# One batch of one-hot rows moved from VectorE to ScalarE, and low products of one layer put last

## The reference

```python
var = jnp.mean(x * x, axis=-1, keepdims=True)
xn = rms_w * (x * jax.lax.rsqrt(var + EPS))
gate = xn @ wg_W + wg_b + (genre_embed @ gg_W + gg_b)
gate_w = jax.nn.softmax(gate, axis=-1)
topk_w, topk_i = jax.lax.top_k(gate_w, TOP_K)
cw = jnp.sum(jax.nn.one_hot(topk_i, E, dtype=x.dtype) * topk_w[..., None], axis=-2)
h1 = jax.nn.relu(jnp.einsum('bsh,ehm->bsem', x, W1) + b1)
h2 = jax.nn.relu(jnp.einsum('bsem,emn->bsen', h1, W2) + b2)
out_e = jnp.einsum('bsen,enh->bseh', h2, W3) + b3
return jnp.einsum('bseh,bse->bsh', out_e, cw)
```

## Time and profile before

| | us |
|---|---|
| median of 3 runs | 443.59 |
| lowest, highest | 442.25, 444.49 |
| profiled execution | 443.45 |
| its span, first to last instruction | 441.5 |
| TensorE busy in it | 406.7 (92%) |
| VectorE, ScalarE, GpSimd busy | 316.5, 294.2, 256.4 |

### The profile page before, as it was taken

One profiled execution on the slowest core, in us unless ns is written; L12 is line 12 of the kernel. 1 busy time (PEld: TensorE's weight loads), 2 busy tenths in 40 slices (PEclk: granted clock), 3 DMA queues, 4 the chain that ended last, 5 costly groups with the idle time before them and its releaser, 6 DMA issues.

```text
span 441.5 us, 12798 instructions
## 1 busy us (share of the span) xinstructions
PE 406.7 (92%) x4134; PEld 365.5 (83%) x4134; DVE 316.5 (72%) x628; ACT 294.2 (67%) x625; POOL 256.4 (58%) x276
## 2 busy tenths in 40 slices
PE   6904989999999999999999999999999999999992
PEld 5604988888888888888888888888888899888891
DVE  3799989849859759769578587555566767776651
ACT  5903798969779789788887865555555556565441
POOL 4740650776676674675656756855556666455324
PEclk9955699999999999999999999999999999999998
DMA  8996499976866756454557454444345443322322
GB/s 281 359 280 208 137 388 383 266 172 167 185 91 158 181 98 150 74 97 70 82 91 171 79 79 74 75 83 76 65 73 78 69 77 71 63 38 37 54 25 33
DMA packets 60968, 57.83 MB, mean 131 GB/s; under 512 B 42059, under 2 KB 55437, under 8 KB 58733
## 3 DMA queue, kind: packets, MB, share of 16 engines
q1 hardware_dynamic: 43072, 38.85, 30.0%
q0 software_dynamic: 13632, 18.00, 25.9%
q10 hardware_dynamic: 4205, 0.17, 0.6%
HBM read 40.08 MB, written 17.83 MB: 131 GB/s over the span
## 4 chain that ended last, share of the span: by engine, by line
PE 68%; ACT 4%; DVE 3%; DMA 3%; issue 2%; POOL 1%; DVEq 1%; POOLq 0%; ACTq 0%
PE bank L1395 49%; PE y_banks L1472 16%; ACT area L837 2%; DMA area<-x_ext,tab_from 2%; PE bank L1375 2%; DVE area L1127 1%; DMA out<-area,tab_to 1%; DVE area L1125 1%; DVE stage L1152 1%; ACT area L863 1%; POOL out L669 1%; PE y_banks L1459 1%; DVEq L1150 0%; ACT w_hi L781 0%; ACT area L851 0%
## 5 line engine op out<-in xcount | busy, mean ns | idle before, releaser
L1395 PE MATMUL bank<-area,w_hi 128*128 128x256 f16 x1248 | 206.3, 273 | 0.0
L1395 PE MATMUL bank<-area,w_lo 128*128 128x256 f16 x624 | 170.1, 273 | 0.0
L669 POOL DMA_INDIRECT out<-area,tab_to x71 | 124.6, 1755 | 63.2 <-issue 22.9
L851 ACT ACTIVATE area<-bank,cprm 128x256 f32<-128x256 f32 (+1 forms) x256 | 127.8, 557 | 43.4 <-PE bank L1395 43.2
L1125 DVE CAST area<-area 128x512 f16<-128x512 f32 (+1 forms) x144 | 65.9, 458 | 95.8 <-ACT area L851 83.6
L1395 PEld LDWEIGHTS bank<-area,w_hi 128*128 (+1 forms) x1248 | 122.1, 98 | 14.3 <-issue 0.2
L631 POOL DMA_INDIRECT area<-x_ext,tab_from x71 | 82.0, 1155 | 52.1 <-issue 36.5
L1127 DVE TENSOR_TENSOR area<-area 128x512 f16<-128x512 f32 (+1 forms) x144 | 99.6, 692 | 5.0
L1472 PE MATMUL y_banks<-w_hi,area 128*128 (+1 forms) x504 | 88.0, 273 | 2.2 <-DVE area L1127 2.2
L863 ACT ACTIVATE area<-area,cw 128x256 f32<-128x256 f32 x71 | 32.2, 499 | 63.3 <-DVE area L1132 44.4
L1472 PE MATMUL y_banks<-w_lo,area 128*128 (+1 forms) x252 | 68.7, 273 | 0.0
(11 more groups left out here) (216 smaller groups left out, 468.0 us busy)
## 6 DMA issues: line engine op xcount, KB each, us to landing
stage<-in_weights SPq DMA_DIRECT2D x10, 1024.0 KB, 5.5
area<-in_x SPq DMA_DIRECT2D x8, 512.0 KB, 8.4
x_ext<-in_x SPq DMA_DIRECT2D x8, 512.0 KB
out<-in_x SPq DMA_DIRECT2D x8, 512.0 KB, 13.1
w_lo<-in_weights SPq DMA_DIRECT2D x4, 1024.0 KB, 8.9
w_hi<-in_weights SPq DMA_DIRECT2D x2, 1024.0 KB, 8.0
area<-x_ext,tab_from POOLq DMA_INDIRECT x71, 3.3
out<-area,tab_to POOLq DMA_INDIRECT x71
```

What stands on the lines that cost most here:

```text
L669: pool.indirect_dma_start(out=out, out_offset=bass.IndirectOffsetOnAxis(ap=tab_to[:, i * SUB + u:i * SUB + u + 1].bitcast(U32), axis=0), i ...
L851: ins = act.activation(to[:, m * T + u * wide:m * T + (u + 1) * wide], ps_h[layer][b][:, a * T + u * wide:a * T + (u + 1) * wide], ACT.Rel ...
L1395: ins = nc.tensor.matmul(out_m, weight, moving, start=(k == 0 and n == 0), stop=(k == chunks - 1 and n == 2))
```

## The change

ScalarE makes the last of the eight batches of one-hot rows. It copies the last eight columns of `row16` to float32 and computes, for each of the eight groups, the square of (row number minus column) from `iota_one` (which counts 0, -1, -2 ...), 128x128 at a time into every eighth element of the batch; one more instruction over 128x1024 turns a square s into relu(1 - s), which is 1 for 0 and else 0. A new semaphore `s_rows` releases it and `s_hot2` tells TensorE. VectorE makes seven batches. In the second part VectorE splits the first half of tile 0's h1 before it makes the low parts of chunk 1 and the second half after them; and TensorE has a function of its own for layer two of tile 0, in which all products with high parts of weights stand before those with low parts, and only the latter wait for `s_low`.

```diff
+            last = hot_r[:, BATCHES - 1]
+            act.wait_ge(s_rows, 1)
+            link(act.activation(row_last, row16[:, (BATCHES - 1) * BATCH:BATCHES * BATCH], ACT.Copy))
+            for n in range(BATCH):
+                ins = act.activation(last[:, :, n], iota_one, ACT.Square, scale=-1.0, bias=row_last[:, n:n + 1])
+            link(ins)
+            act.activation(last, last, ACT.Relu, scale=-1.0, bias=ones32[:, 0:1]).then_inc(s_hot2, 1)
             squares(0)
             squares(1)
...
             link(dve.scalar_tensor_tensor(row16, floor_f, FLOOR_P, slot_f, ALU.subtract, ALU.subtract))
+            dve.sem_inc(s_rows, 1)
...
-            for b in range(BATCHES):
+            for b in range(BATCHES - 1):
                 ns = slice(b * BATCH, (b + 1) * BATCH)
...
-            def split(i, layer):
+            def split(i, layer, parts=(0, 1)):
...
-                for b in range(2):
+                for b in parts:
...
             x_low_first(1)
+            split(0, 0, (0,))
             low_parts(1)
-            split(0, 0)
+            split(0, 0, (1,))
             x_low(1)
...
             for b in range(BATCHES):
-                pe.wait_ge(s_hot, b + 1)
+                if b < BATCHES - 1:
+                    pe.wait_ge(s_hot, b + 1)
+                else:
+                    pe.wait_ge(s_hot2, 1)
...
+            def layer2_first():
+
+                weights, low_weights = owned(0, 1)[0]
+                for u in range(SUB):
+                    pe.wait_ge(s_h1, 1 + u)
+                    for xp, own, first, end in ((h1_hi, weights, True, False), (h1_lo, weights, False, False),
+                                                (h1_hi, low_weights, False, True)):
+                        if end:
+                            pe.wait_ge(s_low, 3)
+                        for m in range(KM):
+                            for k in range(KM):
+                                ins = nc.tensor.matmul(
+                                    ps_h[1][u][:, m * P:(m + 1) * P], own[:, k * M + m * P:k * M + m * P + P],
+                                    chunk_of(xp, KM, k, u), start=(first and m == 0 and k == 0),
+                                    stop=(end and m == KM - 1 and k == KM - 1))
+                    ins.then_inc(s_l2, 1)
```

## The result

The changed kernel took **448.09 us** (median of 5 runs, 447.00 to 451.62) beside 444.49 us (442.25 to 445.26) of the kernel before in the same rounds: a ratio of 1.0083, 95% interval 1.0046 to 1.0120. It is slower, by 3.6 us in the medians and 3.7 by the ratio. The ratio with its interval is worked out from the undisturbed executions alone (the disturbed ones, up to 1011.9 us long, are left out) and is not the quotient of the two medians, from which it lies up to 0.0016 away. The forecast was 443.7, which is 0.1 above the 443.59 of the kernel before at that time, with a range of 442.5 to 445.6. So the time lies outside the range, and there is a loss where next to no change was forecast. The rival that came nearest had a chance of 0.05: ScalarE's writes of one element in eight cost double, 446.2 us.

A forecast was written before the change was run, and what follows sets the result against it. TensorE, busy 92% of the span, was taken as the bound. ScalarE's lateness 0.6 plus part two's 0.3, less 0.76 swallowed at 98.80, left 0.1 us above the 443.59 median: 443.7 us, range 442.5 to 445.6.

The forecast's parts named there:

- Price of ScalarE's eight squares: ScalarE's eight 128x128 squares for the last one-hot batch: 2.6 us, with 2.9 kept as the upper price.
- d: Lateness of the sums, scales, high parts and tile 0 from ScalarE's added batch: 0.6 us, by the upper price 1.0.
- That lateness passes down without slack: From 62 us TensorE, ScalarE and VectorE follow one another without slack to 98 us, except at a 0.76 us wait.
- the idle time ahead of the squares: ScalarE's idle time before 39.80 us, ahead of the weight squares, covers most of the added batch work, not all.
- The last batch is ready before TensorE wants it: ScalarE's batch is ready by 41.0 or 41.4 us, TensorE wants it at 42.8; the table comes 0.2 us earlier.
- Part two costs 0.3 us: Layer two of tile 0: its 48 products end at 62.2 instead of 61.92 us, 0.3 us lost rather than 0.5 saved.
- The wait in the middle: TensorE waits 0.5 us in the middle of tile 0's layer two, after its 32 products without low parts.
- Low parts beside GpSimd's copies: VectorE's low parts take turns with GpSimd's parameter copies and pay 0.7 us; by that rule alone 444.4 us, chance 0.06.
- the cast that had taken 1.24 us: VectorE's cast in splitting h1, taken at 0.42 us; the 1.24 beside GpSimd's copies need not recur.
- TensorE swallows 0.76 us at 98.80: TensorE's 0.76 us wait at 98.80 us absorbs 0.76 of the 0.9 us lateness, leaving 0.1 us.
- The rival of the clock: TensorE's clock rises after layer one's first half in tile 0, 24 products cost more: +1.2 us, 445.0; chance 0.06.
- The rival "slower": ScalarE's writes of one element in eight cost double: eight cost 2.5 us more, +2.6 us in all, 446.2; chance 0.05.

The follow-up runs named there:

- planes: The changed kernel with ScalarE's batch laid out plane by plane, so squares, last instruction and TensorE's reads have neighbouring elements: 442.86 us, ratio 1.0018.
- dummy work: The kernel before with five dummy ScalarE instructions of 128x1024 ahead of the weight squares, all eight batches on VectorE: 447.65 us, ratio 1.0033.
- turned read: The changed kernel with squares written side by side to scratch and reordered by the last instruction's strided read: 447.32 us, ratio 1.0067; again on the third chip 443.85 us, 1.0031.
- part two alone: The kernel before with only the new order of h1's split, low parts and layer two of tile 0: 445.05 us, ratio 1.0000.
- part one alone: The kernel before with only ScalarE making the last one-hot batch: 447.41 us, ratio 1.0063; again on the third chip 444.65 us, 1.0042.
- write forms: The changed kernel with 24 more ScalarE squares of 128x128, four in each of six output forms, ahead of the batch; no kernel time given.
- dummies: The kernel before with three or five dummy ScalarE instructions of 128x1024, all eight batches on VectorE: 446.88 us, ratio 1.0022, and 447.65 us, 1.0033.
- turned read, part one alone: The kernel before with only ScalarE's last batch added, squares side by side in scratch and reordered by the last instruction's read: 447.01 us, ratio 1.0016.
- other order: The kernel before with both h1 halves split before the low parts and all high-weight products first, eight batches on VectorE: 447.11 us, ratio 1.0012.

## Why the prediction was wrong, point by point

- **Price of ScalarE's eight squares: the term that failed.** 2.6 us forecast, "strided 2-byte writes appear in no ScalarE row; I take the 2.6 and keep 2.9"; 5.03 measured, 0.63 us each. The bound above was too near: rows of other layouts can't bound a layout that none of them has. By itself this moves d from 0.6 to 3.0, and 2.84 was measured. The cause is the write: with the outputs side by side the same squares took 2.45, and with planes the lateness and the loss went. The rule of the Trainium skill ("ScalarE: Activation LUTs", What ACT_TABLE_LOAD costs) gave 2.4 us as an estimate, and with neighbouring elements it holds: 2.45 measured. That rule has no term for the step of an output.
- **That lateness passes down without slack.** Right. The dummy work shows it without any batch: d = 1.94 gave 1.5 us. Also right was that the idle time ahead of the squares hides part of the work: the prediction's own terms put the gap at 3.4 us (3.95 us of work for d = 0.6), and 3.5 was measured.
- **The last batch is ready before TensorE wants it.** Wrong with the double writes (TensorE waited 0.44 us, and VectorE's next table instruction 1.32 in place of 0.23). With planes TensorE had no such wait, and that instruction came at 42.08, 4.60 us behind the first product in place of 4.99: 0.4 us earlier, where 0.2 was forecast.
- **Part two costs 0.3 us.** The wait in the middle was forecast at 0.5 and measured at 0.73, with 2.77 us for the pair of low parts in place of 2.47 (in the second profile of the changed kernel 0.58, with 2.62). From the sums to the end of layer two, part two adds 0.57 (planes), 0.27 and 0.79 (turned read, two executions), 0.94 and 0.71 (the changed kernel, two executions) and 0.99 us (part two alone); without it the same stretch is 0.03 us longer, and 0.09 and 0.15 shorter. So 0.3 to 1.0. Alone it can't be told from zero in the time. Beside part one the ratios 1.0066 and 1.0042 are 1.1 us apart, but their intervals overlap and the medians differ by 0.2 us (444.83 and 444.65), so that it costs time is not shown.
- **Low parts beside GpSimd's copies.** The rule of the Trainium skill ("SBUF — State Buffer", Who interferes with whom), that such instructions of VectorE and GpSimd take turns, was given 0.7 us. Both were slower where they met: the low parts by 0.30 us, GpSimd's pair of copies 2.02 us, against 0.77 in the run of part one alone, where they don't meet. The trace agrees with the direction; VectorE paid less than half of the estimate. The prediction's other choice here was right: the cast that had taken 1.24 us beside the copies took 0.41 to 0.43 once it stood elsewhere.
- **TensorE swallows 0.76 us at 98.80.** Right, and shown four times in the table: 0.92, 0.93, 0.92 and 0.92 us came back, and the wait was gone. The table's row of planes is the kernel that the prediction had in mind, and the signs that it named for being right are there: squares 0.31 us apart, a wait for the sums of 2.13 us (2.1), a wait in the middle of layer two, the end of layer two at 62.75 when put on the times of before (62.8), and no wait at 98.80. With d = 0.26 and part two 0.6, less 0.9, nothing is left. The forecast of +0.1 us stands beside 1.0018 [0.9995, 1.0040], and is inside; so is a loss of up to 1.8 us.
- **The rival of the clock.** It is not the loss. In the changed kernel's first profile TensorE's granted clock rose from 0.50 (1.2 GHz) to 1.00 (2.4 GHz) at about 52.2 us, before layer one of tile 0 (53.03), as in before. In its second profile it rose at about 53.6, 0.6 us into layer one (53.05), and two triples of products took 0.32 us each in place of 0.17: 0.3 us, where the rival had 1.2. Some of the 0.94 us above may be this.
- **The rival "slower".** It named the right mechanism and place: d = 3.1 (2.84 measured), part two 0.3, less 0.76, +2.6 us. Measured were 2.9 us by the ratio (1.0066 x 442.6 less 442.6) and 2.2 in the medians on the third chip, without the late signal in the profile, and 3.7 and 3.6 in the first measurement. What was wrong was its chance of 0.05, with "no row speaks for it, none excludes it". A price that nothing excludes, and that makes a loss out of no change, deserved a wider range.

**What stays open** is the late signal. ScalarE's wait for it at the same step of tile 3 was 5.51 us (after), 5.28 (part one), 2.46 (part two), 4.37 (turned read), 5.08 (write forms), 2.33 and 5.35 (dummies), 5.38 (turned read, part one alone) and 5.41 (other order): in every profiled execution on the first two chips of the experiments and in the changed kernel's profile. On the third chip it was absent four times out of four, though three of those kernels are among these. So neither part makes it. Where it occurs the last matmul is later: part one alone ends 395.20 + 5.93 us behind the first product with it, 395.20 + 1.72 without; the changed kernel 395.20 + 6.60 with it, 395.20 + 2.56 without. The unprofiled runs don't show in how many of them it occurs. The kernel before was 2.4 and 3.6 us slower on the first two chips than on the third, so it may occur there too and cancel in the ratios; no profile of it was taken there. Nor is 1.0083 clear of 1.0066, since the intervals overlap. What delays the signal was not found.

## What to carry to other kernels

Price an instruction by its access pattern, not only by engine and element count: before work moves to another engine, look for a row of that engine with the same step and element size, and if there is none, measure it or let the range hold a factor of two. Work that is handed to an idle engine must fit the gap ahead of that engine's next step on the path; here the gap took 3.5 us and the batch needed 6.4. And a layout that suits one producer can be changed for one batch alone: by planes the same work cost ScalarE 3.8 us instead of 6.4, and no loss clear of the noise was left, though nothing was won.

## What was not expected of the hardware

- ScalarE, 128x128: 0.31 to 0.32 us each with two-byte outputs side by side (eight in 2.45, four in 1.28), 0.33 with steps of 4 bytes, 0.36 with steps of 8, **0.60 to 0.67 with two-byte outputs 16 bytes apart**; 0.32 and 0.35 for four-byte outputs side by side and 16 bytes apart. A two-byte read of 128x1024 with 16-byte steps took 2.22 us in place of 1.15.
- In one step of tile 3 ScalarE got TensorE's signal some 4.5 us later (103.25) than by its distance in another execution of the same kernel (an estimate, 98.71), in every profile on two chips and in none on a third.
- The same kernel before took 442.6, 445.0 and 446.2 us on three chips, a spread of 0.8%, as large as the effect that was studied.
